# Putting fills and turns off in TensorE's order by a model of VectorE's load

## The reference

```
x  = L0_attn_query
xn = _layernorm(x);  s = _L0_attn_ref(xn, ...);  g = _silu(_L0_ffn_ref(xn, ...));  x = x + s * g
xn = _layernorm(x);  s = _L1_attn_ref(xn, ...);  g = _silu(_L1_ffn_ref(xn, ...));  x = x + s * g
xn = _layernorm(x);  s = _L2_attn_ref(xn, ...);  g = _silu(_L2_ffn_ref(xn, ...));  x = x + s * g
xn = _layernorm(x);  s = _L3_attn_ref(xn, ...);  g = _silu(_L3_ffn_ref(xn, ...));  x = x + s * g
```

## Time and profile before

| | us |
|---|---|
| three runs | 4335.2, 4350.31, 4353.88 (median 4350.31) |
| the profiled execution, and its span | 4340.05, 4338.3 |
| PE busy | 3676.8 (85%) |
| VectorE busy | 2654.2 (61%) |
| ScalarE busy | 2162.1 (50%) |
| reduces of the fills (L1299), 2064 of them | 1265.1, idle before them 648.3 |
| exponentials (L1266), 2432 | 1120.2, idle before them 1117.6 |
| products of the fills (L1237), 2304 | 788.0, idle before them 129.0 |

### The profile page before, as it was taken

One profiled execution on the slowest core, in us unless ns is written; L12 is line 12 of the kernel. 1 busy time (PEld: TensorE's weight loads), 2 busy tenths in 40 slices (PEclk: granted clock), 3 DMA queues, 4 the chain that ended last, 5 costly groups with the idle time before them and its releaser, 6 DMA issues. The chain is left out here.

```text
span 4338.3 us, 74730 instructions
## 1 busy us (share of the span) xinstructions
PE 3676.8 (85%) x27576; PEld 2093.1 (48%) x27576; DVE 2654.2 (61%) x5949; ACT 2162.1 (50%) x4948; POOL 832.3 (19%) x1043
## 2 busy tenths in 40 slices
PE   5988978889989987998998999878877977887887
PEld 3655644444445543333433334455545655554565
DVE  5667656565656546767766767556546655654665
ACT  3555544555554452755655646544443544444354
POOL 1111010000000003142222321223204202320421
PEclk8999988999998897999998989989989998998999
DMA  3221211111011112111110101102303120230301
GB/s 108 61 50 39 74 40 26 43 28 42 18 43 28 23 45 59 25 32 42 31 38 17 47 22 23 40 23 60 78 9 77 29 57 23 59 78 7 79 21 47
DMA packets 146014, 183.19 MB, mean 42 GB/s; under 512 B 29972, under 2 KB 99796, under 8 KB 142324
## 3 DMA queue, kind: packets, MB, share of 16 engines
q1 hardware_dynamic: 136676, 166.73, 15.3%
q10 hardware_dynamic: 8976, 11.68, 1.1%
HBM read 91.69 MB, written 34.08 MB: 29 GB/s over the span
## 5 line engine op out<-in xcount | busy, mean ns | idle before, releaser
L1266 ACT ACTIVATE prob<-ps_st 128x512 f32<-128x512 f32 (+3 forms) x2432 | 1120.2, 512 | 1117.6 <-PE ps_st L1208 571.6
L1299 DVE TENSOR_REDUCE mhalf<-mx 128x1 f32<-128x512 f32 (+3 forms) x2064 | 1265.1, 653 | 648.3 <-PE mx L1237 324.0
L1237 PE MATMUL mx<-ks,qs 72*128 72x512 bf16 (+3 forms) x2304 | 788.0, 370 | 129.0 <-DVE g_tok L1891 52.5
L1205 PE MATMUL ps_st<-qs,ks 75*128 75x512 bf16 (+3 forms) x2432 | 777.5, 354 | 65.3 <-ACT prob L1266 44.9
L1188 PE MATMUL ps_o<-prob,vst 128*32 128x512 f32 (+3 forms) x5376 | 582.9, 516 | 0.1
L1237 PEld LDWEIGHTS mx<-ks,qs 72*128 72x128 bf16 x2304 | 230.6, 102 | 558.1 <-DVE mhalf L1299 186.0
L1205 PEld LDWEIGHTS ps_st<-qs,ks 75*128 75x128 bf16 x2432 | 242.2, 101 | 325.0 <-ACT prob L1266 168.7
L3119 ACT ACTIVATE pr<-ps,nm,lrq 128x128 f32<-128x128 f32 x512 | 227.0, 463 | 47.5 <-DVE nm L3184 47.5
L1349 POOL COPY vst<-v_tok 128x256 f32<-128x256 f32 x48 | 19.9, 418 | 1196.8 <-PE ps_o L1188 1195.6
L1188 PEld LDWEIGHTS ps_o<-prob,vst 128*32 128x32 f32 x5376 | 114.3, 111 | 179.8 <-ACT prob L1266 82.6
L2122 POOL TENSOR_SCALAR ffn_small<-bcs,table 80x128 f32<-80x128 f32 x256 | 149.1, 600 | 121.7 <-PE mx L2250 114.4
(11 more groups left out here) (452 smaller groups left out, 6382.3 us busy)
## 6 DMA issues: line engine op xcount, KB each, us to landing
qs<-q_scr SPq DMA_DIRECT2D x279, 96.0 KB
ks<-k_scr SPq DMA_DIRECT2D x135, 192.0 KB
lkt<-o SPq DMA_DIRECT2D x224, 64.0 KB, 2.0
lve<-lv SPq DMA_DIRECT2D x24, 512.0 KB, 4.9
tabs<-local_tables SPq DMA_DIRECT2D x4, 2048.0 KB, 8.4
lqt<-o SPq DMA_DIRECT2D x128, 64.0 KB, 2.4
lqt<-o ACTq DMA_DIRECT2D x128, 64.0 KB, 2.1
k_scr<-part SPq DMA_DIRECT2D x30, 256.0 KB, 3.1
```

The lines of the kernel that those rows point to most:

```text
L1205: last = nc.tensor.matmul(ps_st[:, u % 3, 0:q1 - q0], ks[g % 2][0:KR, h, kt * P:(kt + 1) * P], qs[g % 2][0:KR, hf, h, q0 - hf * HALF:q1 - ...
L1237: last = nc.tensor.matmul(bank[:, j * w:(j + 1) * w], qs[g % 2][0:R, hf, h0 + j, (t - 4 * hf) * P:(t - 4 * hf + 1) * P], ks[g % 2][0:R, h0 ...
L1266: nc.scalar.activation(prob[:, b % PROBS, h, 0:q1 - q0], ps_st[:, u % 3, 0:q1 - q0], ACT.Exp, scale=scale).then_inc(S["exped"], 1)
L1299: nc.vector.tensor_reduce(mhalf[:, hf, h0:h0 + heads, t - 4 * hf, part], bank[:, 0:heads * (k1 - k0)].rearrange("p (n w) -> p n w", n=head ...
```

## The change

`paced` (new) goes through the ring in order of planned time and keeps, beside it, a model of VectorE: when it will be free, after the work that the feed-forward classes and arrivals now list in `loads()` (time and duration), and after reading each bank, which takes `READ[kind]` from 0.4 after the item's start. An item of `side` starts no earlier than the modelled read of the item four ahead of it, but at most 3.0 later than planned, and fills and "max" no later than `turn_max_at(e) + 1.5`. The times of the feed-forward items are left as they are, except that successive "outp" of `MoeFfn` stand 0.75 apart or more in the ring's order, and its tensor work is limited by `by`. Scores, values, the copies, the DMAs' times and NEG keep theirs. `slot`, `place` and `by` follow from the new times.

```
+READ = {"fill": 0.70, "max": 2.4, "out": 0.75, "turn": 0.8, "plain": 0.7, "sin": 0.76, ...
+        "out_mm": 0.7, "logits": 0.2, "cum": 2.0, "disp": 0.35, "bc": 0.7, "outp": 1.1, "comb": 0.36, ...}
+def paced(side, steps, loads, latest):
+    ring = sorted([(at, 0, i) for i, (at, *_) in enumerate(side)] + [(at, 1, i) for i, (at, *_) in enumerate(steps)])
+    loads = sorted(loads)
+    finished, out, free, last = [], [None] * len(side), -1e9, -1e9
+    for n, (at, which, i) in enumerate(ring):
+        _, kind, e, k = (side, steps)[which][i]
+        start = max(at, finished[n - RING] if n >= RING else at)
+        if which == 0:
+            start = max(last, min(start, at + 3.0))
+            if kind in ("fill", "max"):
+                start = min(start, latest(e) - (0.05 if kind == "fill" else 0.0))
+            last = start = max(last, start)
+            out[i] = (start, kind, e, k)
+        while loads and loads[0][0] <= start + 0.4:
+            when, cost = loads.pop(0)
+            free = max(free, when) + cost
+        if kind in READ:
+            cost = READ[kind]
+            free = max(free, start + 0.4) + cost
+            finished.append(free)
+        else:
+            finished.append(start + 1.2)
+    return out
@@ attention_layer
+    for r in range(rows):
+        ffns[r].clock = clock
     side = sides()
     for r in range(rows):
-        ffns[r].clock = clock
         ffns[r].plan()
-    ring = sorted(side + [item for r in range(rows) for item in steady(ffns[r].turns())], key=lambda item: item[0])
+    steps = [item for r in range(rows) for item in steady(ffns[r].turns())]
+    side = paced(side, steps, [load for f in (*ffns, *arrivals) for load in f.loads()], lambda e: turn_max_at(e) + 1.5)
+    ring = sorted(side + steps, key=lambda item: item[0])
@@ Arrival
+    def loads(self):
+        at = self.time(self.first)
+        return [(at - 7.0, 1.7), (at - 4.0, 0.9)] + [(max(self.time(self.first + 0.3 + 0.08 * t), self.free + 0.4 * t), 0.28) for t in range(NT)]
...
@@ MoeFfn.turns, MoeFfn.tensor
-        return out
+        after, last = [], -1e9
+        for at, kind, e, n in out:
+            after.append((max(at, last), kind, e, n))
+            last = max(at, last) + (0.75 if kind == "outp" else 0.0)
+        return after
...
-                    yield self.out_at(k, i) + 0.25 * t
+                    yield self.by(self.out_at(k, i) + 0.25 * t, "outp", self.row, u)
```

More of the change, by code:

```diff
@@ L745, in turns, with loads @@
         return super().turns(clock) + [(self.time(self.first + 0.8 + 0.15 * i), "plain", self.row, i) for i in range(2)]
+    def loads(self):
+        at = self.time(self.first)
+        return [(at - 9.0, 1.7), (at - 5.0, 0.8), (at - 2.0, 0.9)] + [(self.time(self.first + 0.3 + 0.04 * t), 0.28) for t in range(NT)]
     def transfers(self, sp):
@@ L944 @@
 RING = 4
+READ = {"fill": 0.70, "max": 2.4, "out": 0.75, "turn": 0.8, "plain": 0.7, "sin": 0.76, "cos": 0.76, "lin": 0.7, "v": 0.7, "ctx": 0.7,
+        "out_mm": 0.7, "logits": 0.2, "cum": 2.0, "disp": 0.35, "bc": 0.7, "outp": 1.1, "comb": 0.36, "gate_t": 0.7, "base": 0.7, "mm_v": 0.7}
+def paced(side, steps, loads, latest):
[21 more added lines that the diff above has]
+    return out
 def attention_layer(net, mode, scale, proj, ffns, arrivals=(), departures=()):
@@ L1564, in plan, with loads @@
         pass
+    def loads(self):
+        if self.row == 0:
+            return []
+        return [(self.at(9.0), 1.3), (self.at(9.01), 1.3)] + [(self.at(10.0 + 0.5 * i), 0.78) for i in range(4)] + [(self.at(15.0 + i), 0.7) for i in range(2)]
     def k_at(self, i):
@@ L1701, in of, with loads, more_loads @@
         return n + self.row * self.counts.get(name, 0)
+    def loads(self):
+        if self.row == 0:
+            return []
+        at = self.route_at + 3.6
+        return [(at + 0.8 * i, 0.25) for i in (1, 2, 5, 6, 7)] + [(at + 6.4, 0.7), (at + 8.0, 0.7)] + [(at + 9.6 + 1.2 * i, 0.55) for i in range(4)] + self.more_loads()
+    def more_loads(self):
+        return []
     def route_memory(self, cut):
@@ L1827, in gate_at, with more_loads @@
         return y if self.row == 0 else self.route_at + 18.5
+    def more_loads(self):
+        return [(self.gate_at(15.5), 3.0)]
     def base_at(self, y):
@@ L2048, in plan, with more_loads @@
             self.route_at = self.clock.at(self.begin + 1.0)
+    def more_loads(self):
+        return [(self.step_at(14.0), 0.4), (self.step_at(17.0), 1.6)]
     def step_at(self, y):
```

## The result

The changed kernel takes 4441.64 us (median of 4 runs, 4435.5 to 4456.68) beside 4349.17 for the kernel before (4335.2 to 4353.88). The ratio is 1.0218, with a 95% interval of 1.0191 to 1.0244: 2.2% slower, 92 us. I had forecast 4371, slower by 21 us, in a range to 4404.

A forecast was written before the change was run, and what follows sets the result against it. PE, working in written order and busy 88 to 92% of the attention stages, was taken to set the pace. Idle +17 and clock +9 on 4340 gave 4366, expected as 4371 beside the runs' mean; range 4326 to 4404.

The forecast's parts named there:

- (1): Stages A to C: fills wait less for their banks' reduces (mhalf); -11 us in B, -2 in A, 0 in C.
- (2): FFN output banks that VectorE reads late: of g_tok's 52.5 us in B -3, of tabs' 17.7 in C nothing.
- (3): Between last fill and turned maximum, PE's stops for mrow: +15 us in A, -5 in B, 0 in C.
- (4): Less PE work from maximum to first scores, so waits there: +13 us in A, +14 in B, +1 in C.
- (5): Later outputs delay normalisation in A and a few in B, +3 us; shorter stops for ScalarE in A, -8.
- (6): TensorE's granted clock falls after new stops: 0.55 us lost per us of idle time, +9 us, bounds 0 and +30.
- the maxima's chain without relief: Rival: ScalarE's stops stay, waits around maxima cost 41 us, room gives back 5 only; 4406 us, chance 0.15.
- room wins: Rival: half of the loads' 178.5 us of mhalf waits goes, 58 us for PE; 4306 us, chance 0.22.
- signs of being right: A: mrow 20 us or more, DMA over 12, 20-35 longer; B: mhalf 20-30, DMA threefold; C within a fifth.

The follow-up runs named there:

- a_max3: The kernel before with stage A's turned maxima 3.0 us later in the plan, fills and all else as before; 4442.3 us, ratio 1.0211.
- a_max: The kernel before with stage A's turned maxima 1.5 us later in the plan, fills and all else as before; 4368.8 us, ratio 1.0035.
- a_fills: The kernel before with only stage A's fills, outputs and turns put off by the model, maxima where they were; 4388.2 us, ratio 1.0115.
- cap1: The changed kernel with the cap on delays at 1.0 us instead of 3.0; 4390.4 us, ratio 1.0108 to the kernel before.

## Why the prediction was wrong

The direction was right, and so were the place (stage A) and two mechanisms there, the maximum's wait and the one behind it. A third, the relief at ScalarE, had the wrong sign, and with it the size failed: the sum had +17 of idle time and +9 of clock, and the trace has +55 and +40. By its steps:

(1) Room for the reduces: forecast -11 in B, -2 in A, 0 in C. In B the loads' waits for mhalf fell by 7.6 us and in C they stayed, about as said; in A they rose by 7. So what B gained A lost, and the relief is nothing in all: A to C have 178.5 us of such waits before and after (16.6 + 32.2 + 129.7 after).

(2) FFN outputs: g_tok 52.5 and 53.5, tabs 17.7 and 17.5. Right.

(3) The maximum's wait in A, forecast +15, measured +20.6. Here a term was mispriced: batches with an output between last fill and maximum were to wait +0.2 each, +4 together. In 13 batches that output's turn now stands directly ahead of the maximum, as at 202.35 above, and VectorE's 0.6 us for it comes before mrow: stops of 1.15 to 1.75 us, 17 of the 29.1 us. The eleven batches with one score and nothing else, 0.9 each and 11 together by the forecast (11 x 0.9 is 9.9), wait 0.64 to 0.92, 8.5 together. In B the stops fell by 17.5, not 5 (the longest from 6.6 to 1.6).

(4) Behind the maximum: forecast +13 in A and +14 in B, measured +19.8 and +15. In C +1 forecast, 11.0 to 13.8 measured. Near enough, and a_max3 shows that this distance does run out; a_max shows that the maximum's own 1.5 us would not have done it alone.

(5) Side effects and relief: the step with the wrong sign. I took -8 for ScalarE's stops in A, half of the 17.3 us and no count, on the argument that ScalarE catches up while PE stops. They grew by 8.7, to 26.0: 16.7 us off, the largest term that was mis-sized. Other stops in A that the sum had at nothing, before:

```profile
PE mx L1237 <- DMA ks<-k_scr: 7.3, 5, 2.3
PE mx L1237 <- ACT stream L1634: 5.1, 3, 1.7
PE mx L1237 <- ACT stream L1638: 4.0, 3, 1.3
PE mx L1253 <- ACT stream L1634: 3.2, 3, 1.1
PE mx L1654 <- ACT stream L1638: 1.1, 3, 0.4
```

The four for the FFN's ScalarE outputs, 13.4 us at fills, turns and products, became 16.8, all at fills. Those for keys in flight, 7.3 us, are gone, a relief that I had not seen. a_fills shows all three with the maxima in place. That what is put off by 3 us then meets scores and FFN products that stay where they were is my reading of it, not shown apart. So the 21 us by which A's idle time exceeds the forecast (42.4 beside 21, side effects included) are 16.7 for prob, 6.8 from (4), 5.6 from (3), 3.4 for the FFN's outputs and 2 from (1), less 7.3 for the keys and some 4 of small rows; the rows of waits leave 2 us over. B is 12 us over (+6.8 beside -5), where the gain at mrow and the loss at the DMA nearly cancel and stops for prob grew from 3.4 to 9.0, and C 4.

(6) The clock: 0.69 us per us of idle time by the stages before, 0.55 taken; over the whole kernel it was 40 / 55 = 0.73. The first figure was the better one. With 55 us of idle time and 0.69, the sum would have been 4340 + 55 + 38 = 4433, which is the measured span. By stage the ratio is no constant: in the variants of stage A it goes from 0.2 (cap1: 28 of idle, 6 of clock) to 1.2 (a_max: 7 and 9), and the variants with 20 us or more of stops for the DMA have 29 or more of clock, those with under 6 have under 14. That the DMA's stops cause the fall is not shown apart from the length of the shift. The length of a stop matters, but doesn't settle it either. In stages A to C of before, 5 of 56 stops of 0.5 to 1.0 us that began at a granted clock of 1.00 had a stretch at the lower level (1.2 GHz) within the next 4 us, 16 of 50 of 1.0 to 1.4, 25 of 36 of 1.4 to 2.5 and all 9 longer ones; but A has 22 stops of 1.4 us or more with the change and 19 in a_fills, beside 9 before, and the clock takes 36.6 and 13.4 us.

The rival that came nearest is the maxima's chain without relief, 4406, with a chance of 0.15: its conditions (mrow and DMA in A past 45 us together; 50.5 measured) came true, and its own price was short for the same reasons, the outputs' turns ahead of the maxima and ScalarE's stops, which it held only unchanged. The range ended at its price. The rival in which room wins is out, by (1) (half of 178.5 times two thirds is 59.5, not 58, which changes nothing). Of the signs of being right, those for mrow, the DMA and the clock in A, for g_tok and the DMA in B and for the lengths of B and C came true, and three did not: mhalf in B came to 32.2, not 20 to 30, the DMA's stops in C grew by a quarter, and stage A by 79 us instead of 20 to 35.

## What to carry to other kernels

A delay that is capped is a shift wherever the model behind it is overfull; compare the model's total load with the stretch it plans for (480 us in 476 here) before reading what it does to single items, and take each price from the trace by shape (0.55 us, not 0.70). An item put off crosses whatever was fitted to stand beside it: for each moved item look at the wait on either side of it, and at what its reader must do first, since two delays in one chain, each alone with under 6 us of stops at the first scores, had 21 together. A relief for which no row stands should enter a sum as zero with a bound, not as a credit; and price a stop with what the clock took per idle microsecond in the trace, here 0.7 over the kernel, with wide bounds for a single stage (0.2 to 1.2).

## What I had not expected of the hardware

Stage B with one and the same order of instructions took 949.4 to 968.1 us, with idle time equal to 3 us: with that order the granted clock moves the length of a stretch by 2% between executions, while whole runs of the kernel before lay between 4328 and 4373. And more short stops go with a lower clock over the whole stage: in a_max3 those for prob fell from 17.3 to 13.2 us, those for the DMA, of 0.2 to 3.2 us, rose to 54.9, and PE's busy time grew by 44.6 us with 50.4 us more of idle time.
